# Fused cross-attention and BitNet FFN on Trainium2: four stages of the FFN moved by one or two half steps

## Chip, cores and metric

One core of one Trainium2 chip runs the whole program. The metric is device time in microseconds (us) of one execution, the median of the runs shown. Lower is better.

## What is computed

64 sequences of 128 tokens, 256 features wide, each with a context of 128 tokens of 192 features. First a cross-attention with 16 heads of 64, whose projections carry low-rank additions; the last 4 context tokens have a softmax of their own. Then an FFN whose two products use quantised activations and ternary weights, with a depthwise convolution of three taps over the tokens and a SiLU between them. Both are added to x:

```python
q_in = x @ Wq + _lora(x, q_down, q_up, q_alpha)
out = _attention(q_in, k_in, v_in) + IPA_SCALE * _attention(q_in, ipa_k, ipa_v)
return out @ Wo + bo + _lora(out, o_down, o_up, o_alpha)
...
scale = 127.0 / jnp.clip(jnp.max(jnp.abs(x), axis=-1, keepdims=True), 1e-05)
xq = jnp.clip(jnp.round(x * scale), -128, 127) / scale
...
h = bit_linear(x, w1)
h = depthwise_conv1d(h.transpose(0, 2, 1), conv_w, conv_b).transpose(0, 2, 1)
return bit_linear(jax.nn.silu(h), w2)
...
x = x + xattn(_layernorm(x), ctx_768)
x = x + ffn(_layernorm(x))
```

## The kernel before

The work goes in 16 groups of four sequences (512 tokens). Attention of a group has 16 chunks, each one sequence and four heads. An iteration has 32 halves, numbered n, two for each chunk. Each engine has its own instruction stream, written out by one function `steps(g, n)` per engine, and the streams meet through semaphores alone. So the order on each engine is fixed by the table of numbers at lines 53 to 83: a stage runs at the half that its number names. In iteration g an engine does attention of group g, `project` of group g with n + 32 and of group g+1 with n (its layer norm and its Q, K and V banks), and `finish` of group g-2 with n + 32 and of group g-1 with n (the FFN). A number of 32 or more thus lies in the next iteration: 37 is half 5 of it.

An attention step stands in each even half. On TensorE it has four parts: `p_v` (L442, the output of the chunk three steps back), the transposes of the probabilities (L451, two steps back), the scores (L464) and the output product (L477, four steps back). VectorE adds up the chunk before (SU, L800, RC, L802) and takes the maxima of the new scores (MX, L805, L806; L808). ScalarE copies outputs and transposed probabilities (L644, L646, L638) and takes the exponentials (L652, L655). GpSimd multiplies by the reciprocals (L1028) and subtracts for the second half of a split output (L1054). There is one PSUM bank for scores and one for transposed probabilities, so the scores of a chunk wait for the exponentials of the one before.

Q (L407), K (L416) and V (L426) use two PSUM banks in turn. Q and K banks are emptied by ScalarE (L619, L620, L625), the first V half by VectorE (L793), the second by ScalarE (L631).

The FFN of a group has one PSUM bank, psF, for everything:

- The quantised input is transposed (L489), its scales are broadcast (L495).
- Eight tiles of the first product (L504), at the halves `M_F1 + M_TILE[j]`. A tile needs the bank emptied by VectorE's multiplication (L868). A tile then passes ScalarE (L673, the middle tap, `M_LAG[0]` halves later), VectorE (L859 and L853, the outer taps), ScalarE (L678, tanh) and VectorE (L873).
- The row maxima of the hidden values in two halves of two instructions (L878, `M_HMAX`), their transposes (L509, `M_HT`), reduction and scales (L882 to L766), and the broadcast of the scales (L514, `M_BC2`).
- The hidden values are scaled and rounded in four pairs of tiles (L889, L893; `M_Q2 + Q2_PLACE[k]`). ScalarE copies the residual into the output tile (L663, `M_COPY`).
- The second product in two parts (L525, `M_F2`), the final sum on VectorE `M_FIN` halves after each (L818). The second part needs the bank that the first sum has read.

```python
j = tile_at(n - M_F1)
...
pe.wait_ge(g_done, g.count(CT, j))
...
if n == M_F2[c] + M_FIN:
    dve.wait_ge(f2_full, g.count(2, c + 1))
```

Within one half VectorE does its attention step first, then the FFN of group g-2, then `project`, then the FFN of group g-1; in the latter the order is final sum, residual, L853, L859, L868, L873, maxima, scales, pairs.

Of the kernel before, what the change touches and what calls it, by code (L numbers as in the profile page):

```python
# [58 lines left out]
N_KI = 10  # L59
N_Q = ((10, 17, 24, 31), (12, 20, 27, 34))  # L60
N_K = ((11, 18, 26, 33), (13, 21, 28, 35))
N_V = ((15, 22, 29, 36), (16, 23, 30, 37))
TERNARY = 5
TERNARY_SUM = TERNARY + 4
M_FIN = 2
EARLY_HALVES = N_XT + 2

M_X2 = (6, 7)
# [2 lines left out]
M_ABS, M_SCALE = 10, 11  # L71
M_QT, M_BC1 = 12, 14
M_F1 = 15
M_TILE = (0, 1, 3, 4, 6, 7, 9, 10)
M_LAG = (1, 1, 2, 3, 3)
M_HOFF = 4
M_HMAX = M_F1 + M_TILE[-1] + M_HOFF
M_HT, M_BC2 = M_HMAX + 2, M_HMAX + 3
M_Q2 = M_HMAX + 4
M_F2 = (M_HMAX + 9, M_HMAX + 11)  # L80
M_COPY = M_Q2 + 2
Q2_PLACE = (0, 0, 1, 2)
FINISH_HALVES = M_F2[1] + M_FIN + 1

# [23 lines left out]
def quad_at(n, places):  # L109
    return places.index(n) if n in places else None  # L110

def tile_at(n):
    return M_TILE.index(n) if n in M_TILE else -1

# [21 lines left out]
def program(nc, x, ctxT, cipaT, Wq, Wk, Wv, Wo, bo, q_downT, q_up, k_downT, k_up, v_downT, v_up, o_downT, o_up,  # L137
            alphas, Wk_ipa, Wv_ipa, w1T, conv_w, conv_b, w2T, out):
    with ExitStack() as ctx:
# [167 lines left out]
        def _(sp):  # L307
# [5 lines left out]
            def project(g, n):  # L313
# [9 lines left out]
                if n == N_KI:  # L323
                    sp.wait_ge(c_split, g.count(1, 1))
                    i = g.off if g.reg is None else g.reg + g.off
                    sp.dma_start(RRAW[:, 0:PAIRS * NB * IPA], kipa_dram[i]).then_inc(ki_in, 16)
                q = quad_at(n, N_V[0])
                if q is not None:
# [54 lines left out]
        def _(pe):  # L383
# [6 lines left out]
            def project(g, n):  # L390
# [7 lines left out]
                for a in range(2):  # L398
# [11 lines left out]
                    if q is not None:  # L410
# [6 lines left out]
                        m.then_inc(unit_full, 1)  # L417
                    q = quad_at(n, N_V[a])
                    if q is not None:
# [183 lines left out]
        def _(act):  # L603
            def project(g, n):
# [9 lines left out]
                for a in range(2):  # L614
# [7 lines left out]
                    if q is not None:  # L622
# [3 lines left out]
                                       ACT.Identity).then_inc(unit_free[u % 2], 1)  # L626
                q = quad_at(n - 1, N_V[1])
                if q is not None:
# [28 lines left out]
            def finish(g, n):  # L657
                if n == M_QT + 1:
                    act.wait_ge(q1t_full, g.count(1, 1))
                    act.activation(Q1T[:].rearrange("p k t -> p (k t)"), psF.bitcast(BF16), ACT.Identity).then_inc(q1t_done, 1)  # L660
                if n == M_COPY:
                    act.wait_ge(q2_done, g.count(CT, NB))
# [74 lines left out]
        def _(dve):  # L737
# [18 lines left out]
            def scales(g, i, clip, levels, worth):  # L756

                step = lambda k: dve.wait_ge(quant[i], g.count(3, k))
                step(1)  # L760
                dve.tensor_scalar(AM[i][:], AR[i][:], clip, None, ALU.max).then_inc(quant[i], 1)
                step(2)
                dve.tensor_scalar(AD[i][:], AM[i][:], worth, WD[:, i:i + 1], ALU.mult, ALU.mult)
                dve.reciprocal(AR[i][:], AM[i][:]).then_inc(quant[i], 1)
                step(3)
                dve.tensor_scalar(AS[i][:], AR[i][:], levels, None, ALU.mult).then_inc(scale_done, 1)  # L766

            def project(g, n):
# [16 lines left out]
                if n == N_XT + 1:  # L785
                    for k in range(2):
                        dve.wait_ge(xt_high, g.count(2, k + 1))
                        dve.tensor_tensor(XT[1][:, k, :], psU[k], XT[0][:, k, :].bitcast(F32), ALU.subtract).then_inc(unit_free[k], 1)
                q = quad_at(n - 1, N_V[0])
                if q is not None:  # L790
# [20 lines left out]
            def finish(g, n):  # L811
                for c in range(2):
                    if n == M_F2[c] + M_FIN:
                        dve.wait_ge(f2_full, g.count(2, c + 1))
# [65 lines left out]
                if n == M_HT:  # L880
                    dve.wait_ge(ht_full, g.count(1, 1))
                    dve.tensor_reduce(AR[1][:], psF.rearrange("p (b c) -> p b c", b=NB), AX.X, ALU.max).then_inc(quant[1], 1)  # L882
                    scales(g, 1, 2 * CLIP, 127.0, 1.0 / 254.0)
                pairs = [k for k in range(CT // 2) if n == M_Q2 + Q2_PLACE[k]]
                for j in (2 * k + i for k in pairs for i in range(2)):
# [108 lines left out]
        def _(pool):  # L994
# [13 lines left out]
            def project(g, n):  # L1008
                if n == N_POW:
                    pool.wait_ge(ln1_var, g.count(1, 1))  # L1010
                    pool.tensor_tensor(RS[0][:], VE[0][:], HALF[:], ALU.pow).then_inc(ln1_rstd, 1)
                q = quad_at(n, N_V[0])
                if q is not None:
# [95 lines left out]
```

## Time and profile before

| | |
|---|---|
| median of 3 runs | 1586.54 us (1584.3 to 1588.57) |
| profiled execution | 1588.63 us |
| its span, first to last instruction | 1586.8 us |
| mean granted TensorE clock | 0.974 |
| TensorE busy | 1441.7 us, 91% |
| VectorE busy | 1181.1 us, 74% |
| ScalarE busy | 1189.0 us, 75% |
| GpSimd busy | 668.0 us, 42% |

The profiled execution's time holds 1.8 us around its span. Busy shares are means over the whole span; start-up with the weights, the repeating middle and the end differ. In the rows further down a time is counted from the span's start, and "[0.79 <-DVE GBS L868]" means that the engine was idle for 0.79 us before this instruction and that VectorE's instruction of line 868 ended it. GBS holds the FFN tiles behind the bank, HP the hidden values, PS is PSUM.

### The profile page before, as it was taken

How to read it: one execution, taken by the hardware profiler on the slowest of the kernel's cores; microseconds unless marked ns; L12 is line 12 of the kernel's file. 1: busy time of each engine (PE TensorE's matmuls, PEld its weight loads, DVE VectorE, ACT ScalarE, POOL GpSimd, SP SyncE). 2: the span in 40 equal slices, each digit the busy share in tenths (PEclk: the TensorE clock that was granted, in tenths of full speed). 3: DMA queues.
4: the chain of work that ended last, by engine and by line, in shares of the span. 5: the costliest groups of instructions: out<-in, count | busy, mean ns of one | idle time of the engine just before them, and what ended most of it. 6: DMA issues, size and time to landing. Idle time of an engine off the chain costs nothing.

```text
span 1586.8 us, 33414 instructions
## 1 busy us (share of the span) xinstructions
PE 1441.7 (91%) x10732; PEld 1182.3 (75%) x10778; DVE 1181.1 (74%) x3061; ACT 1189.0 (75%) x3909; POOL 668.0 (42%) x1053
## 2 busy tenths in 40 slices
PE   6999999999999999999999999999999999998752
PEld 3678778777887878788787877788777877787531
DVE  4254578687878868786877868787887868686866
ACT  2477787877879797887878787787978788786721
POOL 0134444443445444444445444444544444444500
PEclk9899999999999999999999999999999999999865
DMA  7400000001010100001010000001010000100000
GB/s 197 123 29 16 30 2 30 29 26 31 14 42 14 42 1 27 29 14 42 14 42 8 21 27 27 29 14 42 14 42 0 27 29 14 42 1 28 1 14 13
DMA packets 41128, 47.13 MB, mean 30 GB/s; under 512 B 3008, under 2 KB 35200, under 8 KB 41088
## 3 DMA queue, kind: packets, MB, share of 16 engines
q1 hardware_dynamic: 40032, 45.82, 9.5%
q10 hardware_dynamic: 1056, 0.81, 0.2%
q8 instruction: 22, 0.36, 0.1%
q14 instruction: 18, 0.15, 0.0%
HBM read 36.13 MB, written 10.49 MB: 29 GB/s over the span
## 4 chain that ended last, share of the span: by engine, by line
PE 51%; DVE 26%; ACT 14%; issue 8%; DMA 0%; DVEq 0%; POOL 0%; ACTq 0%; POOLq 0%
PE PS L464 8%; PE PS L407 6%; PE PS L477 6%; PE PS L451 5%; PE PS L442 5%; ACT SM L652 5%; PE PS L416 5%; DVE GBS L878 5%; PE PS L426 5%; PE PS L525 3%; PE PS L504 2%; DVE HP L873 2%; DVE GBS L868 2%; DVE GBS L889 2%; DVE MX L806 2%
## 5 line engine op out<-in xcount | busy, mean ns | idle before, releaser
L1028 POOL TENSOR_TENSOR SM<-SM,RC 128x496 f32<-128x496 f32 (+1 forms) x512 | 326.0, 658 | 764.7 <-DVE RC L802 764.7
L652 ACT ACTIVATE SM<-PS,MX 128x124 f32<-128x124 f32 x1024 | 359.0, 364 | 170.0 <-DVE SM L808 166.0
L464 PE MATMUL PS<-KT,QM 128*128 128x128 f32 x2048 | 273.3, 277 | 4.0 <-ACT SM L652 3.8
L464 PEld LDWEIGHTS PS<-KT,QM 128*128 128x128 f32 x2048 | 250.5, 193 | 6.2 <-ACT SM L652 3.4
L1054 POOL TENSOR_TENSOR OTl<-OF,OTh 128x256 fp32r<-128x256 f32 x256 | 208.9, 816 | 22.5 <-ACT OF L646 22.2
L652 ACT ACTIVATION_READ_ACCUMULATOR SM<-PS,MX 128x1 f32 x1024 | 210.2, 205 | 0.0
L451 PE MATMUL PS<-IDF,SM 128*128 128x128 f32 x1024 | 168.9, 288 | 7.0 <-POOL SM L1028 7.0
L644 ACT ACTIVATE OTh<-PS 128x256 fp32r<-128x256 f32 x256 | 99.1, 387 | 101.6 <-PE PS L442 100.5
L806 DVE TENSOR_REDUCE MX<-PS 128x4 f32<-128x496 f32 x256 | 170.2, 665 | 0.0
L442 PE MATMUL PS<-PT,V 128*64 128x128 f32 x2048 | 168.8, 286 | 0.1
L442 PEld LDWEIGHTS PS<-PT,V 128*64 128x64 f32 x2048 | 106.9, 136 | 76.7 <-issue 69.5
L638 ACT ACTIVATE PT<-PS 128x512 f32<-128x512 f32 x256 | 156.3, 611 | 0.7 <-PE PS L451 0.7
L451 PEld LDWEIGHTS PS<-IDF,SM 128*128 128x128 f32 x1024 | 107.9, 141 | 51.5 <-issue 42.7
L868 DVE TENSOR_TENSOR GBS<-PS,BC 128x512 f32<-128x512 f32 x128 | 88.0, 688 | 66.9 <-PE PS L504 66.9
L805 DVE TENSOR_REDUCE MX<-PS 128x4 f32<-128x16 f32 x256 | 40.8, 159 | 118.8 <-PE PS L464 118.7
L477 PE MATMUL PS<-WOh,OTh 128*128 128x256 f32 x512 | 124.3, 324 | 3.6 <-POOL OTl L1054 3.6
L859 DVE SCALAR_TENSOR_TENSOR HP<-GBS,CW,HP 128x508 f32<-128x508 f32 x128 | 96.9, 757 | 38.6 <-ACT HP L673 38.6
L853 DVE SCALAR_TENSOR_TENSOR HP<-GBS,CW,HP 128x508 f32<-128x508 f32 x128 | 120.9, 944 | 1.2
L673 ACT ACTIVATE HP<-GBS,CB,CW 128x512 f32<-128x512 f32 x128 | 111.3, 869 | 12.3 <-DVE GBS L868 10.6
L504 PE MATMUL PS<-Q1T,W 128*128 128x512 bf16 x210 | 70.4, 400 | 48.4 <-DVE GBS L868 36.5
L407 PE MATMUL PS<-XTh,WQh 128*128 128x512 f32 x256 | 105.3, 411 | 0.4
L477 PE MATMUL PS<-WOl,OTh 128*128 128x256 f32 x512 | 103.3, 284 | 0.0
(139 smaller groups left out, 3563.9 us busy)
## 6 DMA issues: line engine op xcount, KB each, us to landing
XIN<-in_x SPq DMA_DIRECT2D x16, 512.0 KB, 3.5
XRES<-in_x SPq DMA_DIRECT2D x16, 512.0 KB, 4.5
out_y<-HP SPq DMA_DIRECT2D x16, 512.0 KB, 3.2
CRAW<-in_ctxT SPq DMA_DIRECT2D x16, 256.0 KB, 2.7
RRAW<-in_ctxT SPq DMA_DIRECT2D x32, 128.0 KB, 2.8
QM<-in_Wq SPq DMA_DIRECT2D x1, 1024.0 KB, 10.7
GBS<-in_Wo SPq DMA_DIRECT2D x1, 1024.0 KB, 21.8
k_ipa_columns<-HP SPq DMA_DIRECT2D x1, 1024.0 KB, 5.1
```

What stands on the lines that cost most here:

```text
L407: m = mm(bank, WQ[w][:, k, P * tile:P * tile + P], XT[xt][:, k, :], start=(i == 0), stop=(i == 5))
L442: m = mm(psO[r:r + DH, h // 2, :], V[:, b, DH * (4 * q + h):DH * (4 * q + h) + DH], PT[:, h, :], start=True, stop=True)
L451: m = pe.transpose(psT[:, h, :], SM[c % 2][:, h, :], IDF[:])
L464: m = mm(psS[:, h, :], QM[:, 2 * q + h // 2, h % 2, TOK * b:TOK * b + TOK], KT[:, 2 * q + h // 2, b, :], start=True, stop=True)
L477: m = mm(psY[b // 2][:, b % 2, :], OT[ot][c % 2][:, a, :], WO[w][:, 2 * q + a, :], start=(q == 0 and i == 0 and b % 2 == 0), stop=(q == QU ...
L638: act.activation(PT[:], psT, ACT.Identity).then_inc(pt_done, 1)
L652: m = act.activation(SM[s % 2][:, h, 0:ORG], psS[:, h, 0:ORG], ACT.Exp, bias=MX[s % 2][:, h:h + 1], accum_out=SU[s % 2][:, h:h + 1])
L806: dve.tensor_reduce(MX[s % 2][:, 0:4], psS[:, :, 0:ORG], AX.X, ALU.max, negate=True)
L853: dve.scalar_tensor_tensor(out=y[:, :, 0:TOK - 1], in0=GB[j % 4][:, :, 1:TOK], scalar=CW[:, j, 2:3], in1=y[:, :, 0:TOK - 1], op0=ALU.mult, ...
L868: dve.tensor_tensor(GB[j % 4].rearrange("p b t -> p (b t)"), psF, BC[:], ALU.mult).then_inc(g_done, 1)
L1028: m = pool.tensor_tensor(part, part, RC[c % 2][:, 4 * i:4 * i + 4].unsqueeze(2).broadcast_to(shape), ALU.mult)
L1054: pool.tensor_tensor(OT[1][c % 2][:], OF[:], OT[0][c % 2][:].bitcast(F32), ALU.subtract).then_inc(ot_done, 1)
```

## The change

Only the table of numbers changes.

```diff
-N_V = ((15, 22, 29, 36), (16, 23, 30, 37))
+N_V = ((15, 22, 29, 36), (16, 23, 30, 38))
-M_FIN = 2
+M_FIN = 1
-M_TILE = (0, 1, 3, 4, 6, 7, 9, 10)
+M_TILE = (0, 1, 3, 5, 6, 8, 9, 11)
-M_COPY = M_Q2 + 2
-Q2_PLACE = (0, 0, 1, 2)
+M_COPY = M_Q2 + 3
+Q2_PLACE = (0, 1, 1, 2)
```

Tiles 3, 5 and 7 of the first product move one half later. Through `M_TILE[-1]` all that follows the tiles moves by one half too: the maxima from halves 29 and 30 to 30 and 31, their transposes from 31 to 32, the broadcast from 32 to 33, the second product from 38 and 40 to 39 and 41. With `M_FIN` of 1 the final sums stay at halves 40 and 42, and so does the output transfer. The four pairs move from 33, 33, 34, 35 to 34, 35, 35, 36, the residual's copy from 35 to 37. The second half of the last V bank moves from half 37 to 38.

On TensorE, from the last product of the attention step at half 20 on, before:

```order
L477 MATMUL PS<-WOh,OTl 128x256 x2
L407 MATMUL PS<-XTh,WQh 128x512
L407 MATMUL PS<-XTl,WQh 128x512
L407 MATMUL PS<-XTh,WQl 128x512
L407 MATMUL PS<-XTh,WQh 128x512
L407 MATMUL PS<-XTl,WQh 128x512
L407 MATMUL PS<-XTh,WQl 128x512
L416 MATMUL PS<-CTh,WKh 128x512
```

and now:

```order
L477 MATMUL PS<-WOh,OTl 128x256 x2
L407 MATMUL PS<-XTh,WQh 128x512
L407 MATMUL PS<-XTl,WQh 128x512
L407 MATMUL PS<-XTh,WQl 128x512
L407 MATMUL PS<-XTh,WQh 128x512
L407 MATMUL PS<-XTl,WQh 128x512
L407 MATMUL PS<-XTh,WQl 128x512
L504 MATMUL PS<-Q1T,W 128x512 x2
L416 MATMUL PS<-CTh,WKh 128x512
```

Tile 3 (two matmuls at L504) stood ahead of this attention step, directly behind tile 2; it now stands between the Q and the K bank.

On VectorE, around the end of an iteration (halves 28 to 31; L129 is the loop's own), before:

```order
L873 SCALAR_TENSOR_TENSOR HP<-GBS,HP 128x512
L878 TENSOR_REDUCE GBS<-HP 128x128 x2
L800 TENSOR_REDUCE SU<-SM 128x4
L802 RECIPROCAL RC<-SU 128x8
L804 REGISTER_ALU
L805 TENSOR_REDUCE MX<-PS 128x4
L806 TENSOR_REDUCE MX<-PS 128x4
L808 TENSOR_TENSOR SM<-PS,MX 128x4x4
L792 REGISTER_ALU
L793 COPY V<-PS 124x2x256
L878 TENSOR_REDUCE GBS<-HP 128x128 x2
L882 TENSOR_REDUCE AR<-PS 128x4
```

and now:

```order
L793 COPY V<-PS 124x2x256
L878 TENSOR_REDUCE GBS<-HP 128x128 x4
L129 REGISTER_ALU
L129 COMPARE_AND_BRANCH
L800 TENSOR_REDUCE SU<-SM 128x4
L802 RECIPROCAL RC<-SU 128x8
L805 TENSOR_REDUCE MX<-PS 128x4
L806 TENSOR_REDUCE MX<-PS 128x4
L808 TENSOR_TENSOR SM<-PS,MX 128x4x4
L882 TENSOR_REDUCE AR<-PS 128x4
```

The four maxima stand together, and the statistics of the next iteration's first chunk now stand between them and the reduction of L882.

On TensorE, halves 5 to 8 of an iteration, before:

```order
L426 MATMUL PS<-WVRh,CTR 128x256
L426 MATMUL PS<-WVRl,CTR 128x256
L442 MATMUL PS<-PT,V 64x128 x4
L451 MATMUL PS<-IDF,SM 128x128 x4
L464 MATMUL PS<-KT,QM 128x128 x4
L477 MATMUL PS<-WOh,OTh 128x256 x2
L477 MATMUL PS<-WOl,OTh 128x256 x2
L477 MATMUL PS<-WOh,OTl 128x256 x2
L525 MATMUL PS<-W,HP 128x256 x16
L442 MATMUL PS<-PT,V 64x128 x4
```

and now:

```order
L477 MATMUL PS<-WOh,OTl 128x256 x2
L426 MATMUL PS<-WVh,CTh 128x256
L426 MATMUL PS<-WVh,CTl 128x256
L426 MATMUL PS<-WVl,CTh 128x256
L426 MATMUL PS<-WVRh,CTR 128x256
L426 MATMUL PS<-WVRl,CTR 128x256
L426 MATMUL PS<-WVh,CTh 128x256
L426 MATMUL PS<-WVh,CTl 128x256
L426 MATMUL PS<-WVl,CTh 128x256
L426 MATMUL PS<-WVRh,CTR 128x256
L426 MATMUL PS<-WVRl,CTR 128x256
L525 MATMUL PS<-W,HP 128x256 x16
```

The second V half, ten matmuls at L426, stood ahead of this attention step and now stands between it and the first part of the second product.

## Rows read from the trace of the kernel before

**Rows 1.** Windows: us; busy (instructions) of PE, PEld, DVE, ACT, POOL; clock, DMA, GB/s.

```profile
646.36:736.70 90.34, 85.76 (x666) 71.61 (x669) 71.54 (x189) 73.18 (x246) 41.56 (x67) 1.00 0.08 25
659.66:693.26 33.60, 31.89 (x235) 25.74 (x236) 27.74 (x61) 31.35 (x97) 18.76 (x27) 1.00 0.05 17
693.26:727.26 34.00, 31.64 (x261) 27.22 (x260) 29.72 (x88) 24.46 (x89) 14.09 (x23) 1.00 0.06 16
1456.05:1529.47 73.42, 51.57 (x363) 40.53 (x367) 58.31 (x139) 41.83 (x144) 30.54 (x40) 0.85 0.03 11
```

**Rows 2.** Waits on TensorE over the span: us in total, times, longest.

```profile
PE PS L504 <- DVE GBS L868: 36.5, 38, 2.3
PE PS L509 <- DVE GBS L878: 21.2, 16, 10.0
PE PS L525 <- DVE HP L818: 18.4, 16, 1.2
...
PE PS L426 <- ACT KT L625: 7.9, 13, 0.6
```

**Rows 3.** Timeline, TensorE, halves 19 to 22: start, us, instruction, idle before.

```profile
664.91 0.60 PE L504 MATMUL PS<-Q1T,W 128*128 128x512 bf16 x2 [0.79 <-DVE GBS L868]
665.45 0.66 PE L442 MATMUL PS<-PT,V 128*64 128x128 f32 x8
...
671.24 0.66 PE L442 MATMUL PS<-PT,V 128*64 128x128 f32 x8
```

**Rows 4.** Timeline, VectorE: statistics of the chunks at halves 20 and 22.

```profile
668.04 0.16 DVE L800 TENSOR_REDUCE SU<-SM 128x4 f32<-128x16 f32 x1
...
673.24 0.17 DVE L800 TENSOR_REDUCE SU<-SM 128x4 f32<-128x16 f32 x1
```

**Rows 5.** Timeline, ScalarE from half 24 to 28, and TensorE's V at half 29.

```profile
680.07 0.36 ACT L652 ACTIVATE SM<-PS,MX 128x124 f32<-128x124 f32 x1 [0.26 <-DVE SM L808]
...
690.81 0.59 ACT L620 ACTIVATE QM<-PS 64x512 f32<-64x512 f32 x1
...
692.00 0.28 PE L426 MATMUL PS<-WVh,CTh 128*128 128x256 f32 x1
```

**Rows 6.** Timeline, VectorE and TensorE, halves 30 to 34.

```profile
696.84 2.34 DVE L878 TENSOR_REDUCE GBS<-HP 128x128 f32<-128x1024 f32 x2
...
699.23 0.66 PE L509 MATMUL PS<-IDF,GBS 128*128 128x128 f32 x4 [0.55 <-DVE GBS L878]
...
701.19 0.17 DVE L766 TENSOR_SCALAR AS<-AR 128x4 f32<-128x4 f32 x1
...
704.63 0.66 PE L442 MATMUL PS<-PT,V 128*64 128x128 f32 x8
```

**Rows 7.** Timeline, VectorE and GpSimd, halves 33 to 37.

```profile
703.59 2.48 DVE L889 TENSOR_TENSOR GBS<-HP,PS 128x512 f32<-128x512 f32 x4
705.99 1.43 DVE L893 TENSOR_SCALAR HP<-GBS 128x512 bf16<-128x512 f32 x4
...
713.50 0.16 DVE L800 TENSOR_REDUCE SU<-SM 128x4 f32<-128x16 f32 x1
...
713.98 1.19 POOL L1028 TENSOR_TENSOR SM<-SM,RC 128x496 f32<-128x496 f32 x2 [3.63 <-DVE RC L802]
...
716.53 0.73 POOL L1054 TENSOR_TENSOR OTl<-OF,OTh 128x256 fp32r<-128x256 f32 x1
```

**Rows 8.** Timeline, VectorE and TensorE, halves 38 to 40.

```profile
718.14 0.17 DVE L805 TENSOR_REDUCE MX<-PS 128x4 f32<-128x16 f32 x1 [1.44 <-PE PS L464]
...
720.50 0.66 PE L442 MATMUL PS<-PT,V 128*64 128x128 f32 x8
...
725.41 1.92 PE L525 MATMUL PS<-W,HP 128*128 128x256 bf16 x16 [1.19 <-DVE HP L818]
```

**Rows 9.** Timeline, VectorE: the last product of the last group's tiles.

```profile
1558.42 0.69 DVE L873 SCALAR_TENSOR_TENSOR HP<-GBS,HP 128x512 f32<-128x512 f32 x1 [0.16 <-ACT GBS L678]
```

**Rows 10.** Line 853 by source: least, median and greatest ns, first and last start.

```profile
L853 DVE SCALAR_TENSOR_TENSOR HP<-GBS,CW,HP x128: 733/992/1211, 206.6 to 1556.9; 128x508 f32<-128x508 f32 x128
```

## The prediction

> **What bounds the kernel now.** I read the windows first, with the attention steps' starts as bounds. TensorE's start-up apart, the run repeats with a period of 90.34 us, one group of four sequences, and TensorE is busy 85.76 us of it at a granted clock of 1.00 [rows 1]; so at most 4.6 us of a period can be won on it. Then the waits on TensorE by line: nearly all of this idle time is five waits per group, two for VectorE's drain of an FFN tile (L504, 36.5 us in total), one for the row maxima (L509), one for the final sum (L525) and one for ScalarE's copy of a K bank (L426) [rows 2]. The change goes at each of the five. Whether they go depends on the two engines behind them, so I then read the same windows for these: in the 33.6 us of the FFN tiles ScalarE is busy 31.35 us, in the 34.0 us behind them VectorE 29.72 us [rows 1]. TensorE asks for each bank once, and the other two can run about half a chunk ahead or behind; a wait that is removed there tends to come back at the next point where TensorE meets the fuller engine.
>
> **The change, replayed over one period.** I move each instruction to its new place, keep the durations of the rows, and note when each engine would reach four meeting places. Times are of the trace before, in us, and up to tile 2 nothing differs.
>
> Tiles. Before, tile 3 waits 0.79 us with nothing between it and tile 2 [rows 3]; by starts it costs 0.86 us. Now an attention step and a Q bank part them, and that wait is gone. But tile 3 is drained a half later, behind VectorE's softmax statistics of that half: these start at 667.45 instead of 668.04 [rows 4], since the drain ahead of them is gone, and take 1.05 us, then tile 2's last tap runs for 0.92 us, and the drain of tile 3 starts at 669.4. Tile 4 may follow 0.75 us behind a drain's start, so at 670.2, where TensorE is ready at 669.8: a new wait of 0.4 us. The next attention step starts at 670.7, 0.5 us earlier than the 671.24 of [rows 3]. ScalarE's first tap of tile 3, however, now falls behind its exponentials (668.6 to 670.1) and two Q copies (1.2 us), at 671.3. VectorE waits for it until 672.2, and its statistics of the next chunk start at 674.1 instead of 673.24 [rows 4]. From there VectorE has no gap up to the chunk after, whose exponentials start at about 680.57 instead of 680.07. Between 680.07 and the end of its Q copy at 691.40 ScalarE has only some 0.6 us of idle time [rows 5]; the same work from 680.57 on ends at 691.5. The V matmul that waits for this bank stood at 692.00 [rows 5] and may now start at 691.6. So of 1.7 us of waits removed (two by 0.86) 0.4 us are left, and V waits 0.8 us in their place. This is the term that I trust least: with 0.5 us more of slack on ScalarE the gain would be 0.9, with 0.4 less it is nothing.
>
> Row maxima. TensorE's transposes waited 0.55 us for them [rows 6]. Before, two of the four maxima run ahead of the last statistics and two behind; now all four run behind, 1.15 us each. They start at 696.5 (696.84 less 0.35 that is won) and end at 701.1; the transposes sit behind an attention step, at 700.9, and wait 0.25 us. But VectorE does the next chunk's statistics first (1.05 us), then the reduction and the scales. These ended at 701.36, 2.13 us behind the transposes' start, 0.69 of it the transposes themselves, so they take 1.44 us: the scales stand at 703.5. The broadcast that needs them is behind one K bank only and waits 0.6 us; it takes 0.8 us, and the attention step starts at 704.35 instead of 704.63 [rows 6]. 0.3 us ahead.
>
> Second product. VectorE now has these statistics before any of the scaling: they start when the scores are there, 706.5, and then three pairs of the scaling come in a row. Two pairs took 3.8 us, 703.59 to the end of the row at 705.99 [rows 7], so three take 5.7, and with the variance of the next group (0.5) the statistics of chunk 2 start at 713.5. That is where they are now, at 713.50 [rows 7]. TensorE, however, gets there a V half sooner. Before, it spent that time on V's second half and waited for its bank (the 7.9 us at L426 [rows 2]); now V stands one step later. The transposes need GpSimd's product, which starts at 713.98 [rows 7] and is read 1.25 us later: 715.2, where TensorE is ready at 714.3. The scores need the exponentials, 716.2, and the output product needs GpSimd's subtraction, started at 716.53 [rows 7] behind its other work: 717.3. Together some 1.7 us of new waits for the 0.62 removed. V (1.2) and the first half of the second product (1.85) follow, and the next attention step starts at 721.1 instead of 720.50 [rows 8]: here the change is 0.6 us behind.
>
> Final sum. VectorE reads the scores of chunk 3 at 717.4 instead of 718.14 [rows 8], so its chain of normalisation, residual and sums would be 0.7 us earlier at the final sum, but it then needs the scores of chunk 4, there at 723.3: 0.4 us is left. The sum stays in its half; the second part of the product, 1.19 us late before [rows 8], starts at 725.0 instead of 725.41. TensorE is ready at 724.9.
>
> Sum: 0.4 us per group at the point where the lead is carried on; behind it up to the next tile 2 TensorE has only the wait of tile 0 for the broadcast scales, and that moves along. Fourteen groups run under another group's projections: 5.6 us. The nearest rows bound this: at most 3.3 us (the two tile waits, V, the row maxima and half the final one), and below nothing by the 0.6 us by which the second product's step is late, if the final sum does not give it back. I take the replay, with 0.05 to 0.75 as its own width.
>
> Ends. In the last group nothing runs beside the FFN. VectorE's last product waited 0.16 us for ScalarE, since another product stood between [rows 9]; now it follows its tap directly and waits 0.9 us. Likewise the first tap of tile 3 directly behind its drain. By replay 1.2 us, and for the group ahead of it, in a window where TensorE is busy 51.57 of 73.42 us and VectorE 58.31 [rows 1], 0.8 us, as the four maxima stand together behind a later last tile. I add 2.0, between 0 and 4. No DMA moves: the output transfer keeps its half, and the copy of the residual into the output tile, now behind two more exponentials, has 2.6 us until its reader. That costs nothing while ScalarE is idle there.
>
> The profiled execution took 1588.63 us, 2.1 above the median of 1586.54. 1588.6 less 5.6 plus 2.0 is 1585.0, by the median's measure 1583.0.
>
> **A rule weighed.** VectorE's tap with two inputs in SBUF takes 733 ns at least and 992 in the median [rows 10]; the long ones run while GpSimd multiplies. I carry 0.25 us for each, in the replay. The Trainium skill (SBUF — State Buffer, Who interferes with whom) says that such an instruction and a GpSimd one that reads SBUF exclude each other, so that the later one blocks fully. By that rule a tap issued 0.55 us after GpSimd's start would lose the other 0.6 us, not 0.25.
>
> **Rivals.** (1) ScalarE has the slack: V does not wait, since the first tap of tile 3 overtakes or the copies run closer. For it: ScalarE idles 2.3 us in that window [rows 1]. Against: half of this lies ahead of the place. Then 1.0 us per group is won: 14.0 less 2.0, 1574.5. (2) Slower, by the serial chain from the four maxima over scales, broadcast and the three pairs to the statistics of chunk 2. For it: VectorE is the fuller engine there, and every 0.1 us of its lateness reaches TensorE three steps on. It decides from the point where these statistics start over 0.4 us later than 713.5; at 714.6 TensorE gets to the final sum 0.7 us behind, and 9.8 plus 2 us are lost: 1598. Against: VectorE idles about 1.2 us ahead of the scores at 706.5. (3) Taps that follow the statistics directly are one or two more than before, and if each is blocked for the full multiplication, VectorE loses 0.4 us twice in the stretch without gaps, 0.8 us per group, 11 us: 1594. The median of 992 ns speaks against it [rows 10]. By the page's rule above it would come so. (4) The order moves, but every wait is taken over in full: 1586.5 to 1588.5.
>
> **How the numbers follow.** 0.3%, 4.8 us, is about what a measurement of this kernel can tell from no change: faster is below 1581.8, slower above 1591.3. Forecast 0.50, its own range 1578 to 1588; of it 0.20 lies below 1581.8. Rival 1 0.22, rival 2 0.16, rival 3 0.05, rival 4 0.07. Faster 0.42, same 0.37, slower 0.21. The range reaches to rival 1 and to the near end of rivals 2 and 3: 1574 to 1595.
>
> **What would show it.** Right: a period of about 89.95 us; the L504 waits for VectorE down from two of 0.79 to one of about 0.4 per group; V at L426 waiting for the Q copy (L620) instead of the K copy; L514 waiting for L766; new waits at L451, L464 and L477 in half 6; the last wait at L525 nearly gone. Wrong: no V wait at half 29 and a period near 89.3 (rival 1), or chunk 2's statistics late and a period above 90.5 (rival 2); in rival 3 the median of L853 would rise by 100 ns or more.

## The result, and the profile after it

The changed kernel takes 1596.68 us (median of 8 runs, 1594.38 to 1600.94) against 1588.44 us (8 runs, 1584.3 to 1590.33) of the kernel before: a ratio of 1.0057, 95% interval 1.0044 to 1.007. It is slower by 0.6%. The forecast was 1583.0 us, and the range up to 1595 us does not hold the result.

The windows of the changed kernel for one period and for the group ahead of the end, as the first and the last of [rows 1], with the same columns:

```profile
646.24:737.17 90.93, 86.60 (x665) 71.62 (x669) 71.89 (x189) 73.13 (x245) 40.78 (x67) 1.00 0.08 25
...
1461.96:1536.33 74.37, 51.20 (x362) 40.21 (x367) 57.63 (x139) 41.75 (x144) 29.18 (x40) 0.88 0.03 12
```

The period grew from 90.34 us to 90.93, at a full clock as before. The group ahead of the end takes 74.37 us where it took 73.42. The waits on TensorE by line over the span, us in total, times and longest:

```profile
PE PS L451 <- POOL SM L1028: 19.8, 21, 1.4
PE PS L514 <- DVE AS L766: 17.7, 16, 1.9
PE PS L504 <- DVE GBS L868: 17.4, 22, 2.7
...
PE PS L525 <- DVE HP L818: 8.5, 16, 1.0
```

Against [rows 2] the waits for the tiles' drain (L504) and for the final sum (L525) are half gone, as the change meant. Two others stand in their place: TensorE waits at the broadcast for the scales (L514), once in each group, and for chunk 2's probabilities (L451). One period in detail, all labelled waits of TensorE from half 21 on and the steps behind two of them:

```profile
670.04 0.61 PE L504 MATMUL PS<-Q1T,W 128*128 128x512 bf16 x2 [0.24 <-DVE GBS L868]
...
691.38 0.39 PE L426 MATMUL PS<-WVh,CTh 128*128 128x256 f32 x1 [0.52 <-ACT QM L620]
...
703.87 1.16 PE L514 MATMUL PS<-IDF,AS 128*128 128x128 f32 x8 [1.02 <-DVE AS L766]
704.95 0.66 PE L442 MATMUL PS<-PT,V 128*64 128x128 f32 x8
...
715.82 0.66 PE L451 MATMUL PS<-IDF,SM 128*128 128x128 f32 x4 [0.93 <-POOL SM L1028]
716.80 1.16 PE L464 MATMUL PS<-KT,QM 128*128 128x128 f32 x8 [0.33 <-ACT SM L652]
...
721.73 0.66 PE L442 MATMUL PS<-PT,V 128*64 128x128 f32 x8
...
725.88 1.92 PE L525 MATMUL PS<-W,HP 128*128 128x256 bf16 x16 [0.44 <-DVE HP L818]
```

Each of these waits stands at a place where the forecast had one; the two that it had at the maxima's transposes (L509) and at the output product (L477) are not there. The waits of tile 4 and of V are shorter than forecast (0.24 and 0.52 us, forecast 0.4 and 0.8). Then the scales come late. VectorE's row in the same period:

```profile
701.94 0.68 DVE L882 TENSOR_REDUCE AR<-PS 128x4 f32<-128x512 f32 x1
702.65 0.61 DVE L761 TENSOR_SCALAR AM<-AR 128x4 f32<-128x4 f32 x1
703.30 0.23 DVE L763 TENSOR_SCALAR AD<-AM,WD 128x4 f32<-128x4 f32 x1
...
707.13 0.17 DVE L805 TENSOR_REDUCE MX<-PS 128x4 f32<-128x16 f32 x1 [1.68 <-PE PS L464]
...
714.10 0.16 DVE L800 TENSOR_REDUCE SU<-SM 128x4 f32<-128x16 f32 x1
...
718.77 1.98 DVE L752 TENSOR_SCALAR XIN<-XIN,MV,RS 128x256 f32<-128x256 f32 x4
...
724.96 0.86 DVE L818 SCALAR_TENSOR_TENSOR HP<-PS,AD,HP 128x256 f32<-128x256 f32 x2
```

and the timeline of GpSimd at that place:

```profile
702.51 0.73 POOL L1054 TENSOR_TENSOR OTl<-OF,OTh 128x256 fp32r<-128x256 f32 x1
```

L761, an instruction on four elements per partition, takes 0.61 us; in the kernel before it took 172 ns at most. It ends at 703.26, and GpSimd's subtraction, which began 0.14 us ahead of it, at 703.24. It is so in 14 of the 16 groups (0.59 to 0.65 us); in the fifteenth, where the subtraction starts 0.06 us behind it, and in the last, where there is none, it takes 0.17. L752 stands 1.98 us where it took 1.37 in the kernel before; beside it GpSimd now works without a gap from 718.20 to 720.27, where before its work ended 0.2 us behind the start of L752. And VectorE has no gap left: between the scores of chunk 1 and the final sum it is busy 17.51 us of 17.83,

```profile
707.13:724.96 17.83, 17.51 (x57) 1.00 0.10 30
```

(the window of that stretch, VectorE's busy time alone, clock, DMA), where in the kernel before it was busy 14.83 of 17.69, and idled 1.07 and 1.44 us:

```profile
706.80:724.49 17.69, 14.83 (x56) 1.00 0.11 31
```

The page's chain of work that ended last says the same in shares of the span, for the changed kernel

```profile
DVE 35%; PE 33%; ACT 20%; issue 11%; DVEq 0%; DMA 0%; POOL 0%; ACTq 0%; POOLq 0%
```

and for the kernel before:

```profile
PE 51%; DVE 26%; ACT 14%; issue 8%; DMA 0%; DVEq 0%; POOL 0%; ACTq 0%; POOLq 0%
```

A larger share of the path lies on VectorE than on TensorE now, though VectorE's busy time hardly changed (1184.1 us, before 1181.1).

In these two executions the changed kernel is 2.6 us ahead at chunk 9 of the third group (295.5 against 298.1), loses 12 times 0.60 us, and is 5.7 us longer from there to its end: 10.3 us in all, the difference of the spans (1597.2, 1586.8). The medians differ by 8.2 us.

### The profile page after: what moved, and what is told of

Read it like the earlier page. It is cut to its first block, busy times and chain, and to the rows that moved or that the text cites. A ratio compares the mean times of both kernels' runs of the same rounds, so it can differ in the third digit from the quotient of the medians.

```text
span 1597.2 us, 33464 instructions
## 1 busy us (share of the span) xinstructions
PE 1453.8 (91%) x10717; PEld 1182.0 (74%) x10778; DVE 1184.1 (74%) x3061; ACT 1187.5 (74%) x3909; POOL 656.5 (41%) x1053
## 4 chain that ended last, share of the span: by engine, by line
DVE 35%; PE 33%; ACT 20%; issue 11%; DVEq 0%; DMA 0%; POOL 0%; ACTq 0%; POOLq 0%
ACT SM L652 7%; PE PS L464 5%; PE PS L407 5%; DVE GBS L878 5%; DVE GBS L889 4%; PE PS L442 4%; PE PS L451 3%; ACT HP L673 3%; PE PS L416 3%; PE PS L525 3%; DVE HP L859 3%; DVE HP L873 3%; PE PS L477 2%; ACT QM L620 2%; PE PS L426 2%
## 5 line engine op out<-in xcount | busy, mean ns | idle before, releaser
L1028 POOL TENSOR_TENSOR SM<-SM,RC 128x496 f32<-128x496 f32 (+1 forms) x512 | 339.1, 683 | 781.3 <-DVE RC L802 781.3
L464 PE MATMUL PS<-KT,QM 128*128 128x128 f32 x2048 | 276.8, 279 | 7.3 <-ACT SM L652 7.1
L464 PEld LDWEIGHTS PS<-KT,QM 128*128 128x128 f32 x2048 | 251.0, 193 | 14.9 <-ACT SM L652 11.6
L1054 POOL TENSOR_TENSOR OTl<-OF,OTh 128x256 fp32r<-128x256 f32 x256 | 196.2, 766 | 23.8 <-ACT OF L646 23.6
L451 PE MATMUL PS<-IDF,SM 128*128 128x128 f32 x1024 | 169.1, 288 | 20.6 <-POOL SM L1028 19.8
L451 PEld LDWEIGHTS PS<-IDF,SM 128*128 128x128 f32 x1024 | 108.0, 141 | 67.2 <-issue 37.6
L477 PE MATMUL PS<-WOh,OTh 128*128 128x256 f32 x512 | 124.0, 323 | 1.2 <-POOL OTl L1054 1.2
L673 ACT ACTIVATE HP<-GBS,CB,CW 128x512 f32<-128x512 f32 x128 | 110.4, 862 | 13.7 <-DVE GBS L868 11.6
L853 DVE SCALAR_TENSOR_TENSOR HP<-GBS,CW,HP 128x508 f32<-128x508 f32 x128 | 117.8, 921 | 0.1
L873 DVE SCALAR_TENSOR_TENSOR HP<-GBS,HP 128x512 f32<-128x512 f32 x128 | 91.0, 711 | 29.9 <-ACT GBS L678 29.9
L407 PE MATMUL PS<-XTh,WQh 128*128 128x512 f32 x256 | 108.1, 422 | 0.4
L477 PE MATMUL PS<-WOl,OTh 128*128 128x256 f32 x512 | 102.8, 283 | 0.0
```

What stands on the lines that cost most here:

```text
L407: m = mm(bank, WQ[w][:, k, P * tile:P * tile + P], XT[xt][:, k, :], start=(i == 0), stop=(i == 5))
L451: m = pe.transpose(psT[:, h, :], SM[c % 2][:, h, :], IDF[:])
L464: m = mm(psS[:, h, :], QM[:, 2 * q + h // 2, h % 2, TOK * b:TOK * b + TOK], KT[:, 2 * q + h // 2, b, :], start=True, stop=True)
L477: m = mm(psY[b // 2][:, b % 2, :], OT[ot][c % 2][:, a, :], WO[w][:, 2 * q + a, :], start=(q == 0 and i == 0 and b % 2 == 0), stop=(q == QU ...
L673: act.activation(HT[j].rearrange("p (b t) -> p b t", b=NB), GB[j % 4], ACT.Identity, bias=CB[:, j:j + 1], scale=CW[:, j, 1:2]).then_inc(t1 ...
L1028: m = pool.tensor_tensor(part, part, RC[c % 2][:, 4 * i:4 * i + 4].unsqueeze(2).broadcast_to(shape), ALU.mult)
```

## The experiments

The table is the yardstick for all of them. From each trace, in us: the start of the attention steps of chunks 15, 1 and 5 behind that of chunk 9, and the period, each the mean over the same twelve groups. Chunk 15 is read ahead of the row maxima (the FFN tiles' gain stands there), chunk 1 behind the broadcast, chunk 5 behind the final sum. In one period these repeat to about 0.03 us, while the time before the first group's attention lies between 92.9 and 96.1 us in executions with the same order there; so a mechanism is judged by the period, and a version by the measured time. The experiments ran on three chips, each beside the kernel before, whose median there was 1588.0 to 1590.2 us. So two of the times are compared by the ratio in the last column.

| kernel | chunk 15 | chunk 1 | chunk 5 | period | ratio of times to before (95%) |
|---|---|---|---|---|---|
| before | 33.61 | 45.02 | 67.64 | 90.36 | |
| changed | 33.23 | 45.46 | 68.24 | 90.96 | 1.0057 (1.0044 to 1.007) |
| e2_late_stages | 33.60 | 45.70 | 68.49 | 91.21 | 1.0088 (1.0072 to 1.0103) |
| e3_v_half | 33.62 | 45.00 | 67.32 | 90.04 | 0.995 (0.9934 to 0.9966) |
| e5_tiles_3_5 | 33.46 | 45.47 | 68.10 | 90.81 | 1.0048 (1.0031 to 1.0065) |
| e1_tiles_only | 33.22 | 47.17 | 69.80 | 92.51 | 1.0195 (1.018 to 1.021) |
| e4_no_v_half | 33.23 | 45.46 | 68.25 | 90.97 | 1.0074 (1.006 to 1.0088) |
| e6_scales_psum | 33.22 | 45.18 | 67.98 | 90.69 | 1.0041 (1.0026 to 1.0056) |
| g7_all_psum | 33.26 | 45.06 | 67.87 | 90.58 | 1.0033 (1.0021 to 1.0046) |
| g5_var_early | 33.22 | 45.46 | 67.76 | 90.48 | 1.0027 (1.0017 to 1.0036) |
| h1_both_fixes | 33.25 | 45.05 | 67.35 | 90.07 | 0.9999 (0.9988 to 1.001) |
| f3_bc2_later | 33.26 | (order moved) | 69.43 | 92.19 | 1.0173 (1.0158 to 1.0188) |
| f4_pairs_spread | 33.26 | 45.49 | 69.30 | 92.03 | 1.0147 (1.0134 to 1.0161) |
| f1_tile3_v | 35.80 | 47.14 | 69.46 | 92.17 | 1.0147 (1.013 to 1.0165) |
| g6_v_var_early | 33.62 | 45.00 | 67.70 | 90.42 | 0.9992 (0.9983 to 1.0001) |
| h2_v_pair4_later | 33.60 | 45.00 | 66.91 | 89.63 | 0.994 (0.9925 to 0.9955) |

### The change taken apart

**Late stages alone**, against the kernel before:

```diff
-M_FIN = 2
+M_FIN = 1
-M_HOFF = 4
+M_HOFF = 5
-M_COPY = M_Q2 + 2
-Q2_PLACE = (0, 0, 1, 2)
+M_COPY = M_Q2 + 3
+Q2_PLACE = (0, 1, 1, 2)
```

(M_HOFF counts from the last tile; with that tile in its old half, 5 puts the row maxima where the change has them.)

> The stages behind the FFN tiles alone (all four row maxima a half later, three pairs of the scaling in a row, final sum moved), with the tiles and the V half where they were before. Theory A, the loss lies in the serial chain from the maxima over scales and broadcast (the scales stood behind a GpSimd subtraction for 0.44 us, the normalisation behind another GpSimd product for 0.6 us): the 0.4 us that the tiles win per group are missing and the chain's loss stays, so the period is 90.9 to 91.3 us and the time 1595 to 1602 us. Theory B, the parted tiles and the moved V half make ScalarE and VectorE late and this shows only further on: the period is 90.3 to 90.5 and the time 1586 to 1590.

1601.89 us. The loss is all there: 0.68 us at chunk 1, 0.85 at chunk 5. Against it the changed kernel is 0.37 us ahead at chunk 15, and at chunk 1 and 5 only 0.25. Theory A holds; B is out.

**The V half alone:**

```diff
-N_V = (...(16, 23, 30, 37))
+N_V = (...(16, 23, 30, 38))
```

> The kernel before with the second half of V (quad 1, last unit) one half later, nothing else. Theory A: its wait for the K bank (0.6 us per group) goes and comes back as waits in the attention step ahead, since VectorE's statistics of chunk 2 stay where they are; period 90.0 to 90.4, and up to 2 us less at the start; 1583 to 1588. Theory B (V is part of what costs): period above 90.6, 1592 or more.

1581.57 us, 0.5% faster than the kernel before. The period, 90.04, is at the near end of theory A's range; the time lies 1.4 us below it. The K-bank wait (0.61 us) goes, three waits at chunk 2 come (0.41, 0.17, 0.33), and the wait for the final sum falls from 1.19 us to 0.22. TensorE's timeline in it:

```profile
801.35 0.66 PE L442 MATMUL PS<-PT,V 128*64 128x128 f32 x8 [0.41 <-ACT PT L638]
802.17 0.66 PE L451 MATMUL PS<-IDF,SM 128*128 128x128 f32 x4 [0.17 <-POOL SM L1028]
...
812.05 1.92 PE L525 MATMUL PS<-W,HP 128*128 128x256 bf16 x16 [0.22 <-DVE HP L818]
```

In this kernel VectorE waits for the scores of chunk 3 (1.44 us before), so TensorE reaching them earlier lets the whole row behind them start earlier.

**The change without the V half** (M_TILE and the late stages as in the change, N_V as before):

> The changed kernel with the V half back at its old place. Alone, the V half took 0.33 us off each period of 90.36 us. Theory A (the parts add up: tiles -0.4, late stages +0.8, V -0.3 per period, and what is left shows no coupling): period about 91.3 us, 1601 to 1605. Rival (V only pays because the old final sum made TensorE wait 1.2 us; with the late stages of the change it is worth nothing): period 90.9 to 91.0, 1596 to 1598.

1600.98 us, 3 us above the rival's range, but the period, 90.97, is that of the change, and the spans of the two profiled executions differ by only 0.8 us (1598.0, 1597.2): the rival is right by the period, which is what it was about. The same move that is worth 0.33 us per group alone is worth nothing here, since VectorE no longer waits for TensorE in that stretch: the final sum is late instead, and TensorE waits 1.59 us for it. What it still gives it gives once: 0.4 us in the first projections and 1.2 us at chunks 3 to 6 of the second group, ahead of the first FFN tile.

**Tiles 3 and 5, with tile 7 as before:**

```diff
-M_TILE = (0, 1, 3, 4, 6, 7, 9, 10)
+M_TILE = (0, 1, 3, 5, 6, 8, 9, 10)
```

> Tiles 3 and 5 parted as in the change, tile 7, the row maxima and everything behind them where they were before. Theory A: 0.3 to 0.4 us of lead per group at the V matmul, as the changed kernel showed, and no later chain that eats it; period about 90.0, 1582 to 1585. Rival: the lead is lost at the row maxima, since the last tiles' products are late by as much as before: 1588. Theory B (parted tiles cost more further on than they win): period above 90.6, 1592 or more.

1596.47 us, period 90.81: theory A is refuted, and theory B's numbers are met (above 90.6, 1592 or more). The lead is 0.54 us behind tile 3, only 0.15 at chunk 15, and 0.45 us behind at chunk 1. I had overlooked that tiles 5, 6 and 7 now stand in consecutive halves: the last waits 1.19 us for its drain instead of 0.79, and VectorE's copy of the V bank, behind these drains, holds up a Q bank for 0.35. TensorE's waits behind tile 4:

```profile
774.61 0.60 PE L504 MATMUL PS<-Q1T,W 128*128 128x512 bf16 x2 [1.19 <-DVE GBS L868]
...
789.94 0.50 PE L407 MATMUL PS<-XTh,WQh 128*128 128x512 f32 x1 [0.35 <-DVE V L793]
...
792.20 0.66 PE L509 MATMUL PS<-IDF,GBS 128*128 128x128 f32 x4 [0.59 <-DVE GBS L878]
```

**All the tiles of the change, the rest as before:**

```diff
-M_TILE = (0, 1, 3, 4, 6, 7, 9, 10)
+M_TILE = (0, 1, 3, 5, 6, 8, 9, 11)
-M_HOFF = 4
+M_HOFF = 3
```

> The change's tiles with the row maxima and all behind them kept in their old halves, the V half too. The last tile's product then stands directly ahead of the first two maxima (2.3 us), and these ahead of a chunk's statistics. 
1620.64 us. As theory A has it, the last product (L873) waits for ScalarE, then come two maxima, then a chunk's statistics, then the V copy on which TensorE waits. VectorE's timeline:

```profile
795.40 0.69 DVE L873 SCALAR_TENSOR_TENSOR HP<-GBS,HP 128x512 f32<-128x512 f32 x1 [1.98 <-ACT GBS L678]
796.12 2.35 DVE L878 TENSOR_REDUCE GBS<-HP 128x128 f32<-128x1024 f32 x2
798.39 0.16 DVE L800 TENSOR_REDUCE SU<-SM 128x4 f32<-128x16 f32 x1
...
799.44 0.68 DVE L793 COPY V<-PS 124x512 f32<-124x512 f32 x1
```

The wait is 2.04 us at L407; the clock fell behind it in one group of twelve, not in each. In the orders tried in which tiles are parted and the maxima stay (this one, the one ahead and f1_tile3_v below), more was lost than won. With the late stages of the change the price is 0.68 and more.

### The scales behind GpSimd

Against the changed kernel; nothing moves, one small tile is put into the PSUM bank that it is reduced from:

```diff
-        AR = [sb(f"AR{i}", [P, NB]) for i in range(2)]
+        AR = [sb("AR0", [P, NB]), None]
...
         psF = PS[:, 7, :]
+        AR[1] = psF[:, 0:NB]
```

> The changed kernel with the four reduced maxima of the FFN written into the PSUM bank that they are read from, not into SBUF, so that the first instruction of the scales reads PSUM and not SBUF. Nothing else moves. Theory A1 (a one-input instruction from SBUF to SBUF on VectorE stands until the GpSimd instruction that reads SBUF is through, and one that reads PSUM does not): that instruction falls from 0.61 to 0.15 to 0.2 us, the broadcast starts 0.45 us earlier, and the period falls by 0.4 to 0.6 us; 1588 to 1592. Rival A2 (it stands for another reason, its semaphore or the wait behind the reduction, or it stands in this form too): duration about 0.6, 1596 to 1597. Rival A3 (it falls, but the next point, three pairs of the scaling and the statistics of chunk 2, takes the gain): duration 0.2, time 1595 to 1597.

1594.24 us, period 90.70. The first instruction falls to 0.16 us, the next one, now the first that has both sides in SBUF, takes 0.40. VectorE's timeline:

```profile
792.14 0.16 DVE L762 TENSOR_SCALAR AM<-PS 128x4 f32<-128x4 f32 x1
792.34 0.40 DVE L764 TENSOR_SCALAR AD<-AM,WD 128x4 f32<-128x4 f32 x1
```

with GpSimd's subtraction from 791.99 to 792.72. (Lines are one on from here, by the added line.) Theory A1 in kind, but with 0.27 us off the period instead of 0.4 to 0.6, and a time above its 1588 to 1592. The second tile too:

```diff
-        AM = [sb(f"AM{i}", [P, NB]) for i in range(2)]
+        AM = [sb("AM0", [P, NB]), None]
...
+        AR[1], AM[1] = psF[:, 0:NB], psF[:, NB:2 * NB]
```

> The changed kernel with both small tiles of the scales' chain in the PSUM bank, so that none of the chain's instructions reads SBUF alone. With only the first of them in PSUM it took 0.16 us instead of 0.61, but the next, from SBUF to SBUF, took 0.40 instead of 0.23: the GpSimd instruction (0.73 us) had not ended. Theory A (what is held up is the first VectorE instruction that has both sides in SBUF): the second takes about 0.2 to 0.25 too, the broadcast's wait falls from 0.76 to 0.55 us, and the period by another 0.15 to 0.2 us; 1590 to 1593. Rival (any next instruction is held up): times as before it, 1593 to 1596.

Period 90.58, another 0.11 us less where 0.15 to 0.2 were expected; 1594.73 us in the median, above the range. By the time alone this kernel is not told from the changed one (the intervals of the ratios overlap); by the period it is. Nothing is held up any more, though GpSimd runs at the same place; VectorE, and behind it GpSimd:

```profile
789.62 0.17 DVE L762 TENSOR_SCALAR PS<-PS 128x4 f32<-128x4 f32 x1
789.83 0.22 DVE L764 TENSOR_SCALAR AD<-PS,WD 128x4 f32<-128x4 f32 x1
```

```profile
789.47 0.73 POOL L1055 TENSOR_TENSOR OTl<-OF,OTh 128x256 fp32r<-128x256 f32 x1
```

The hold-up is worth 0.38 us of the period, of the 0.60 lost. The Trainium skill (SBUF — State Buffer, Who interferes with whom) says that tensor_scalar can enter a mode that takes the port pair shared with GpSimd, and that the later one then blocks fully, while a VectorE instruction with at most one SBUF input outside such modes does not. The trace agrees: blocked to within 0.02 us of GpSimd's end with both sides in SBUF, unblocked with PSUM as its source (0.17 us).

### The row without gaps

Against the changed kernel:

```diff
-N_STATS, N_VAR, N_POW, N_NORM = 0, 3, 4, 6
+N_STATS, N_VAR, N_POW, N_NORM = 0, 1, 4, 6
```

> The changed kernel with the variance of the next group's first normalisation (0.5 us on VectorE) taken out of the row between the scaling and chunk 2's statistics and put right behind the sums that it reads, where VectorE waits 1.7 us for chunk 1's scores. Theory A (from chunk 1's scores at the row maxima up to the final sum VectorE runs 17.8 us without a gap, and this row sets chunk 2's statistics and the final sum): both come 0.5 us earlier, the period falls by 0.4 to 0.5 us, 1588 to 1591. Rival (TensorE or the broadcast sets the step; 0.5 us less on VectorE only makes a gap): 1595 to 1598.

Period 90.48: the 0.5 us taken out of the row come off the period in full (0.48), and chunk 2's wait at L451 falls from 0.93 to 0.43 us. Theory A by the period. The time, 1593.57 us, is above its range: 14 times 0.48 would be 6.7 us, the medians fell by 3.1 and the ratio by 0.3%, 4.8 us, while the profiled execution was the fastest of ten and its span (1587.7) fell by 9.5. TensorE's wait in it:

```profile
803.73 0.66 PE L451 MATMUL PS<-IDF,SM 128*128 128x128 f32 x4 [0.43 <-POOL SM L1028]
```

Both cures together, in the changed kernel:

> The changed kernel with both small tiles of the scales in PSUM (period 90.58) and the variance early (90.48 alone, against 90.96 of the change). Theory A (both shorten one and the same row of VectorE, from the row maxima to the final sum): the gains add, period 90.1, and with the changed kernel's longer last group 1585 to 1589. Rival (with one of them out of the way TensorE itself sets the step, so that the second brings nothing): period 90.4 to 90.6, 1590 to 1594.

Period 90.07, 1587.29 us: the two add up (0.38 and 0.48 of 0.89). With them the changed order is level with the kernel before (ratio 0.9999), and here the measured time, with an interval far from the changed kernel's, says so too.

### Two attempts to move the chain

Against the changed kernel, the broadcast later, and in another run the pairs of the scaling one to a half:

```diff
-M_HT, M_BC2 = M_HMAX + 2, M_HMAX + 3
+M_HT, M_BC2 = M_HMAX + 2, M_HMAX + 4
```

> The changed kernel with the broadcast of the second product's scales behind the next attention step and Q bank. TensorE no longer waits for the scales (1.0 us per group). Theory A (VectorE's order behind it decides: the three pairs still start at about 0.7 us behind the next row maxima of the scores, and chunk 2's statistics stay at about 12.3 us behind the transposes): the wait comes back at chunk 2's transposes and scores, which grow from 1.3 us to 2.3, and the period changes by 0.2 us at most; 1593 to 1599. Rival (the broadcast's wait itself costs): 0.7 to 1.0 us less per group, 1583 to 1587.

```diff
-Q2_PLACE = (0, 1, 1, 2)
+Q2_PLACE = (0, 1, 2, 3)
```

> The changed kernel with the four pairs of the scaling one to a half (before two, one, one; in the change one, two, one), so that two pairs and not three stand ahead of chunk 2's statistics. Theory A (the serial chain over three pairs makes chunk 2's statistics late): these start 1.9 us earlier, TensorE's waits for them (0.93 and 0.33 us) go, and what is left is set by the final sum, where VectorE has the same work in all; 0.3 to 1.0 us less per group, 1583 to 1592. Rival (the pair moved behind them makes the final sum late by as much): 1595 to 1598.

1617.06 and 1612.88 us: both far outside either theory. In the first the wait did move to chunk 2, as theory A says, but it stands there as one of 2.29 us, and behind it the granted clock was 0.50 (1.2 GHz) for some 3.4 us. In the second the final sum waits 2.4 us in each group; the statistics of chunk 3 now have both last pairs ahead of them. TensorE in the first, at chunk 2:

```profile
720.09 0.66 PE L451 MATMUL PS<-IDF,SM 128*128 128x128 f32 x4 [2.29 <-POOL SM L1028]
```

and in the second, at the final sum:

```profile
730.80 1.92 PE L525 MATMUL PS<-W,HP 128*128 128x256 bf16 x16 [2.39 <-DVE HP L818]
```

**One tile moved, with the V half**, against the kernel before:

```diff
-M_TILE = (0, 1, 3, 4, 6, 7, 9, 10)
+M_TILE = (0, 1, 3, 5, 6, 7, 9, 10)
```

> The kernel before with tile 3 one half later (tiles 4 to 7, the row maxima and all behind them as before) and the V half later. With tiles 3 and 5 moved and three tiles in consecutive halves, the row maxima were 0.6 us late and ate a lead of 0.15. Theory A (each tile that is later makes the chain tile, three taps, product, maxima later; tile 3 alone leaves VectorE time to catch up): 0.1 to 0.5 us of lead per period kept up to the broadcast, period 89.5 to 89.9, 1575 to 1580. Rival (any tile moved makes the maxima late by as much as it wins): period 90.0 to 90.2, 1581 to 1585.

1612.02 us. Tiles 3, 4 and 5 stand in consecutive halves, tile 5 waits 1.93 us for the drain of tile 4, and the clock falls behind it. The timeline, and the windows around it (us, TensorE's busy time, granted clock, DMA share, GB/s):

```profile
686.91 0.60 PE L504 MATMUL PS<-Q1T,W 128*128 128x512 bf16 x2 [1.93 <-DVE GBS L868]
```

```profile
686.00:687.00 1.00, 0.09 (x1) 1.00 0.00 0
688.00:691.00 3.00, 3.00 (x17) 0.50 0.00 0
692.00:698.00 6.00, 6.00 (x42) 1.00 0.12 29
```

### A version that beats both

The V half alone is faster. Two moves on top of it, against e3_v_half. First the early variance, as above:

> The kernel before with the V half later (1581.6 us, period 90.03) and this variance early as well. Theory A: with the V half later, VectorE's row decides here too (TensorE waits 0.41, 0.17 and 0.33 us at chunk 2 and 0.22 at the final sum), so 0.3 to 0.5 us less per period, 1575 to 1578. Rival (here VectorE has no gap ahead of chunk 1's scores to take the 0.5 us, or TensorE sets the pace): 1580 to 1583.

1588.20 us, period 90.42: all of the V half's gain is gone. Behind the old maxima VectorE has no gap ahead of chunk 1's scores, and 0.5 us there makes their statistics 0.6 us late. The same edit that won 0.48 us in the changed kernel costs 0.38 here. Then the last pair of the scaling behind chunk 2's statistics:

```diff
-Q2_PLACE = (0, 0, 1, 2)
+Q2_PLACE = (0, 0, 1, 3)
```

> The kernel before with the V half later (period 90.04) and the last pair of the scaling moved from before to behind chunk 2's statistics. In the trace with the V half later VectorE has 2.0 us of this pair ahead of them, TensorE waits 0.41, 0.17 and 0.33 us at chunk 2, and behind them VectorE idles 1.07 and 0.70 us. Theory A: the three waits go, the idle time takes the pair, and the final sum is up to 1.0 us earlier, period 89.0 to 89.5, 1567 to 1575. Rival (as with the pairs spread in the changed kernel, where TensorE waited 2.4 us for the final sum and the clock fell or the restart cost more): the pair makes the final sum late, period 90.2 or more, 1584 to 1600.

1578.77 us, ratio 0.994, the fastest of all, its own gain over the V half alone 0.41 us per group against 0.5 to 1.0 expected, its time above the 1567 to 1575. Its interval overlaps that of e3_v_half, so by time alone the two are not told apart; by the period they are. TensorE's waits that are left at chunk 2 are those for ScalarE, in its timeline:

```profile
796.00 0.66 PE L442 MATMUL PS<-PT,V 128*64 128x128 f32 x8 [0.41 <-ACT PT L638]
797.57 1.16 PE L464 MATMUL PS<-KT,QM 128*128 128x128 f32 x8 [0.33 <-ACT SM L652]
```

## Why the prediction was wrong

Of the 13.7 us between forecast and result, 1.9 lie in the kernel before, whose median was 1586.54 us in three runs and is 1588.44 in eight. The rest is the change.

**Tiles: right.** Forecast: tile 3's wait gone, tile 4 waiting 0.4 us, V waiting 0.8 us for the Q copy (L620), 0.4 us of lead left. Measured: 0.24, 0.52 and 0.38 us of lead at chunk 15. The rival with ScalarE's slack is out. In part this is luck: the two waits are 0.4 us shorter than forecast, and as much went in gaps too short to be labelled, 0.3 us of it around V's wait and 0.2 ahead of chunk 14.

**Row maxima: the step that failed.** The forecast had the scales 1.44 us behind the transposes' end, by the time they took before, the broadcast waiting 0.6 us and the attention step 0.3 us ahead of the kernel before. The wait was 1.02 us and the step is 0.43 us behind. Of these 0.7 us, 0.44 are L761 held up by GpSimd's subtraction, shown by the two kernels that put its operands into PSUM. The rest is the broadcast: the forecast took 0.8 us from its start to the attention step, read from 702.50 to 703.30 in the kernel before, but there a K bank follows it. From 703.87 to the attention step at 704.95 it is 1.08 us, and the same 1.09 behind the shorter waits of e6_scales_psum and g7_all_psum. By the single records 0.10 of it is the first transpose behind a wait (the second starts 0.21 us behind it, 0.11 without a wait), and 0.18 stands at the seam to the attention step. I had carried the durations of VectorE's small instructions over without asking what GpSimd does in their new place; the rule of the Trainium skill was weighed for the taps alone, where it changed nothing (L853 has a median of 990 ns, before 992), and rival 3 stands refuted.

**Second product: the mechanism right, its start late.** Chunk 2's statistics at 714.10, or 714.2 on the clock of the trace before, against 713.5. The new waits came to 1.3 us rather than 1.7, at L451 and L464, none at L477. The V half, which the forecast let follow for nothing, is worth 0.33 us per group where VectorE has slack and nothing where it has none.

**Final sum: wrong in sign.** I let 0.4 us be won here because VectorE would read the scores of chunk 3 earlier. From chunk 1's scores on VectorE has no gap in the changed kernel, so nothing is given back: the 0.7 us of the scales arrive in full, and 0.3 of the 0.6 by which L752 is longer are added. Forecast 0.4 ahead, measured 0.60 behind.

**Ends: the sum right by luck.** +2.0 forecast between 0 and 4. Measured in one execution of each kernel are 5.7 us lost behind the twelve periods and 2.6 won ahead of them, 3.1 together, of which 1.2 belong to the two of the fourteen groups that lie outside the twelve: 1.9. But this is a balance. The forecast had no gain at the start, where 1.6 us are the V half's and the rest lies within what executions differ by there. At the end the group ahead of the last costs 0.95 us (forecast 0.8) and the last 3.5 (forecast 1.2). In the last, VectorE's work up to the row maxima is 1.4 us longer, much as forecast; the other 2.1 us are the two parts of the last second product. They ran at a granted clock of 0.58 and 1.00 in the kernel before and of 0.50 both in the changed one, a term that the forecast did not have. TensorE's timeline before,

```profile
1576.43 3.21 PE L525 MATMUL PS<-W,HP 128*128 128x256 bf16 x16 [7.90 <-DVE HP L893]
1580.61 1.92 PE L525 MATMUL PS<-W,HP 128*128 128x256 bf16 x16 [0.97 <-DVE HP L818]
```

and in the changed kernel:

```profile
1584.71 3.60 PE L525 MATMUL PS<-W,HP 128*128 128x256 bf16 x16 [7.90 <-DVE HP L893]
1589.28 3.60 PE L525 MATMUL PS<-W,HP 128*128 128x256 bf16 x16 [0.97 <-DVE HP L818]
```

By the medians the whole loss is 8.2 us and 14 times 0.60 is 8.4, which leaves nothing for the ends; so their sum is not settled to better than some 2 us.

So it went by rival 2, the serial chain from the maxima over scales, broadcast and three pairs, which the forecast gave 0.16. It was to decide when chunk 2's statistics are over 0.4 us late; they are 0.7 late, and its price of 1598 us is near the 1596.7 (as a loss, 11.8 us against the 8.2 of the medians; per group 0.7 against 0.60). Against it I set 1.2 us of VectorE's idle time ahead of chunk 1's scores; the idle time is there (1.68 us), but it is a wait for the broadcast and moves with it. What was not tried is to take away the 0.6 us on L752 alone; that GpSimd's work beside it is the cause, and its share of 0.3, are read from the traces and not shown.

## What to carry to other kernels

Ask, for each engine, where its next idle time lies behind the place that you touch: a delay is forgiven there and nowhere earlier, and a gain stops there too, so the same edit won 0.48 us in one order and cost 0.38 in the other. Before work is packed behind a late result, sum it up to the next fixed point: 14.8 us of 17.7 left room, 17.5 of 17.8 turned each tenth into a tenth of the period. And when small instructions are moved, look at what GpSimd does in the new place, and put their operands into PSUM where a bank is at hand.

## What the runs showed of the hardware beside this

A wait of about 2 us is dearer than its length, but not always. Behind 1.93 us (f1_tile3_v) and 2.29 us (f3_bc2_later) the granted clock was 0.50 for some 3.4 us in each of the twelve groups; behind 2.4 us (f4_pairs_spread) in six of twelve, with the same instructions and the same wait in each; behind the 2.04 us of e1_tiles_only in one, for 6.8 us. Behind the 1.59 us for the final sum, in each group of e2_late_stages and e4_no_v_half, it stayed at 1.00, as it did with all shorter waits. Where it fell, the wait cost 1.6 us on top of itself: f1_tile3_v is 0.60 us behind the kernel before at chunk 13, just behind the wait, and 2.19 at chunk 14, with no wait between them. A short wait costs some 0.1 us in the matmul behind it too: in the changed kernel the matmul behind the one that waited at L426 starts 0.22 us later (691.38, 691.60), without a wait 0.12 (692.00, 692.12 in the kernel before). That is not all. In the changed kernel's period the labelled waits are shorter than before (4.0 against 4.5 us), and TensorE is recorded busy 0.84 us longer for the same work; where the rest of that goes is not shown.
